# First operands in blocks, the last residuals of the first layer pair in buffers of their own, and a rearranged end in a two-pair graph kernel

## What is computed

```
x = layernorm(x + L0(x, adj));  out = layernorm(x + L1(x, adj))

L0, for each of 2 layers:
  u   = h (h W_left^T)^T on and above the diagonal, h (h W_right^T)^T below it, / sqrt(384)
  p   = exp(u) * adj;  attention = p / (sum(p) + 1e-10)
  ctx = attention @ (h W_lin^T + b);  h = relu((ctx - mean) / (std + 1e-3) * ln_a + ln_b)
L1, for each of 2 layers:
  a   = softmax(h h^T / sqrt(384)) * adj, divided by its row sum
  ctx = upper(a) @ (h Wl^T + bl) + diag(a) * (h Ws^T + bs) + lower(a) @ (h Wr^T + br)
  h   = relu(normalised ctx * ln_w + ln_b)
```

## Time and profile before

| | us |
|---|---|
| median of 3 runs | 1717.54 |
| range of the runs | 1716.96 to 1718.06 |
| the profiled execution | 1716.51 |
| its span, first to last instruction | 1714.9 |
| TensorE busy in the span | 1667.0 (97%) |
| VectorE busy | 1267.7 (74%) |
| ScalarE busy | 948.4 (55%) |
| GpSimd busy | 614.6 (36%) |

### The profile page before, as it was taken

One profiled execution on the slowest core, in us unless ns is written; L12 is line 12 of the kernel. 1 busy time (PEld: TensorE's weight loads), 2 busy tenths in 40 slices (PEclk: granted clock), 3 DMA queues, 4 the chain that ended last, 5 costly groups with the idle time before them and its releaser, 6 DMA issues.

```text
span 1714.9 us, 29860 instructions
## 1 busy us (share of the span) xinstructions
PE 1667.0 (97%) x9664; PEld 1579.3 (92%) x9664; DVE 1267.7 (74%) x2785; ACT 948.4 (55%) x1985; POOL 614.6 (36%) x658
## 2 busy tenths in 40 slices
PE   7999999999999999999989999999999999999994
PEld 6989989899898889889889999999999999999994
DVE  4587685867859578695876877769687696877866
ACT  4545455464554645546556665655655656656653
POOL 5143252432424233243522523525143351523503
PEclk9999999999999999999999999999999999999997
DMA  7015012020300203003013040300304003030101
GB/s 230 1 32 157 6 48 75 24 92 6 104 19 24 92 6 116 6 24 93 21 61 96 22 95 0 102 15 22 95 3 114 1 22 96 22 95 0 64 14 37
DMA packets 108015, 92.19 MB, mean 54 GB/s; under 512 B 63280, under 2 KB 101168, under 8 KB 107952
## 3 DMA queue, kind: packets, MB, share of 16 engines
q1 hardware_dynamic: 107952, 91.51, 18.6%
HBM read 66.33 MB, written 25.17 MB: 53 GB/s over the span
## 4 chain that ended last, share of the span: by engine, by line
PE 51%; issue 32%; POOL 10%; DVE 3%; ACT 2%; SPq 1%; DMA 1%; POOLq 0%; ACTq 0%; DVEq 0%
PE b_work L1157 34%; PE b_work L1170 8%; POOL g_qv_lo L621 3%; POOL b_ht L601 3%; PE b_score_ps L119 3%; PE b_work L372 2%; PE b_score_ps L386 1%; PE b_work L396 1%; POOL g_keep_l L616 1%; POOL g_sigma L630 1%; POOL g_a_nat L617 1%; POOL g_frstd L634 1%; PE b_turn L1114 1%; PE b_score_ps L1133 1%; PE b_score_ps L1130 0%
## 5 line engine op out<-in xcount | busy, mean ns | idle before, releaser
L1157 PE MATMUL b_work<-b_w_hi,b_ht 128*128 128x384 f32 x2304 | 607.0, 338 | 8.3 <-ACT b_work L1256 8.3
L1157 PEld LDWEIGHTS b_work<-b_w_hi,b_ht 128*128 128x128 f32 x2304 | 418.6, 188 | 10.0 <-ACT b_work L1256 9.4
L1157 PE MATMUL b_work<-b_w_lo,b_ht 128*128 128x384 f32 x1152 | 385.9, 335 | 0.0
L372 PE MATMUL b_work<-b_ht,b_w_hi 128*128 128x512 f32 x1152 | 357.7, 392 | 9.5 <-DVE b_w_lo L696 9.5
L372 PEld LDWEIGHTS b_work<-b_ht,b_w_hi 128*128 128x128 f32 x1152 | 216.3, 189 | 51.2 <-issue 9.5
L621 POOL TENSOR_TENSOR g_qv_lo<-g_v_full,g_qv_hi 128x384 fp32r<-128x384 f32 x128 | 133.4, 1062 | 361.0 <-ACT g_qv_hi L495 361.0
L372 PE MATMUL b_work<-b_ht,b_w_lo 128*128 128x512 f32 x576 | 225.8, 392 | 0.0
L1494 DVE TENSOR_TENSOR s_v_lo<-b_work,s_v_hi 128x384 fp32r<-128x384 f32 x256 | 139.3, 554 | 116.1 <-ACT s_v_hi L1262 114.5
L1157 PEld LDWEIGHTS b_work<-b_w_lo,b_ht 128*128 128x128 f32 x1152 | 217.1, 188 | 0.0
L728 DVE TENSOR_TENSOR g_qv_lo<-b_work,g_qv_hi 128x512 fp32r<-128x512 f32 x192 | 128.8, 687 | 111.1 <-ACT g_qv_hi L483 109.2
L396 PE MATMUL b_work<-b_w_hi,b_ht 128*128 128x384 f32 x768 | 206.2, 336 | 0.0
(11 more groups left out here) (142 smaller groups left out, 3247.6 us busy)
## 6 DMA issues: line engine op xcount, KB each, us to landing
b_x_in<-in_x_t SPq DMA_DIRECT2D x16, 768.0 KB, 7.2
g_x_res<-in_x SPq DMA_DIRECT2D x16, 768.0 KB, 7.5
x<-b_z SPq DMA_DIRECT2D x16, 768.0 KB, 3.9
b_x_in<-x SPq DMA_DIRECT2D x64, 192.0 KB, 6.7
s_x_res<-x SPq DMA_DIRECT2D x16, 768.0 KB, 6.9
out<-b_z SPq DMA_DIRECT2D x15, 768.0 KB, 4.1
b_a_tr<-in_adj_t SPq DMA_DIRECT2D x64, 64.0 KB, 3.4
g_a_nat<-in_adj SPq DMA_DIRECT2D x32, 64.0 KB, 2.4
```

The source lines that it names most:

```text
L372: mm = pe.matmul(bank[:], w, h, start=(n == 0), stop=(n == len(pairs) - 1))
L1157: mm = pe.matmul(bank[:, 0:H], h, w, start=(n == 0 and side == 2), stop=(n == len(pairs) - 1), skip_group_check=True)
```

## The change

On the start: the rows of x and W_left come in three blocks each, alternating, with the constants after W_right; ScalarE and VectorE split them block by block; the first three queries are accumulated side by side in three banks, one block of features after the other; W_right is split in three pieces by columns, and query j of W_right waits for its piece alone. Before that TensorE multiplies a tile of zeros ten times. On the hand-over: both `x_res` of the first block outlive it; the sums of the last pass's residuals go there instead of into `z`, and are normalised and stored from there. The residual of stream 0 leaves VectorE's last unit of the first block, gains, shifts, residuals, statistics, offsets, ScalarE's normalisations, the splits of the three weights and SyncE's stores are moved to other places of the second block's first pass (units 0 to 3). On the end: stream 0's cut, row sums and normalisation are done by ScalarE, its addition, statistics and root by GpSimd; the last unit's contexts and variances are taken in halves; the last stores are three.

```
 start, SyncE
-            load_x(0, 0)
+            for k in range(KO):
+                sp.dma_start(stage[0][:, k], weights[0][k * P:(k + 1) * P]).then_inc(first_in[k], 16)
+                sp.dma_start(xt_in[0][:, k], x_t_v[0, 0][:, k]).then_inc(x_loaded[0] if k == KO - 1 else first_in[k], 16)
             for n, w in enumerate(weights):
-                if n == 1:
+                if n == 0:
+                    continue
+                if n == 2:
                     sp.dma_start(const[:], table).then_inc(const_in, 16)
...
 start, TensorE
-            pe.wait_ge(const_in, 16)
-            query(0, 0, 0).then_inc(work_full, 1 + NT)
-            for j in range(1, QB):
+            def first_queries():
+                banks = [work[query_use(0, m) % RING] for m in range(KO)]
+                for k in range(KO):
+                    for n, (w, h) in enumerate(((w_hi, ht_hi), (w_hi, ht_lo), (w_lo, ht_hi))):
...
+                        for m in range(KO):
+                            mm = pe.matmul(banks[m][:], w[:, 0, 0, k, m * P:(m + 1) * P], h[0][:, k, :],
+                                           start=(k == 0 and n == 0), stop=(k == KO - 1 and n == 2))
...
+            pe.wait_ge(zeros_set, 1)
+            for _ in range(10):
+                pe.matmul(score_ps[:, 0, 0, :], prob[:, 0, :], prob[:, 1, :], start=True, stop=True)
+            first_queries()
+            for j in range(KO, QB):
                 query(0, 0, j).then_inc(work_full, 1)
             value(0, 0, 0)
             scores(0, 0, False)
+            pe.wait_ge(const_in, 16)
 start, ScalarE
             for k in range(KO):
-                turn_out(0, 0, k)
-            weight_hi(0)
-            weight_hi(1)
+                first_hi(k)
+            for m in range(KO):
+                second_weight_hi(m)
+            query_hi(0, 0, 0)
             weight_hi(2)
-            query_hi(0, 0, 0)
             for j in range(1, QB):
                 query_hi(0, 0, j)
                 if j < 4:
                     weight_hi(j + 2)
 hand-over, VectorE, last unit of the first block
                 if not more:
-                    add_residual(i, s)
+                    for t in range(NT):
+                        context_stats(i, unit, t, more)
+                    return
 hand-over, VectorE, first unit of the second block
             biased_value(0, 0, 1)
-            gated.gain_and_shift(0)
+            gated.residual(0, 0)
             biased_value(0, 0, 2)
-            gated.gain_and_shift(1)
...
             biased_value(0, 0, 3)
-            gated.gain_and_shift(2)
+            gated.residual(0, 1)
...
             biased_value(0, 0, 6)
-            gated.residual_and_stats((0,))
+            gated.gain_and_shift(0)
...
             biased_value(0, 0, 11)
-            contexts_out(0, 0)
+            gated.gain_and_shift(1)
+            contexts_out(0, 0, first=True)
 hand-over, VectorE, later units (tail is the unit)
+                    if tail == 1 and j < 5:
+                        gated.gain_and_shift(j - 1)
+                    if tail == 2:
+                        gated.final_stats(0, j - 3)
...
 hand-over, ScalarE
             seed(0, 0, 6)
-            gated_normalise(0)
...
             seed(0, 0, 7)
-            weight_hi(0)
...
             copy_part(0, 1)
+            weight_hi(0)
             weight_hi(1)
...
-                if tail:
-                    gated_normalise(1)
...
-                if tail:
-                    weight_hi(2)
                 if more:
                     copy_part(i, unit + 1)
+                if tail == 1:
+                    weight_hi(2)
+                if tail in (2, 3):
+                    gated_normalise(tail - 2)
 hand-over, SyncE
             sp.wait_ge(folded, 1)
-            store_last(0)
             load_weight(0)
             load_weight(1)
             sp.wait_ge(split, 1)
             load_weight(2)
-            store_last(1)
...
                         load_adj(i + 1, s)
+                    if first:
+                        store_last(s)
 end, GpSimd
+            def last_steps(i):
+                s = STREAMS - 1
+                other_residual(i, (0, 1, 2))
+                half_roots(i, 0)
+                other_residual(i, (3,))
+                times_gain(i, s, 0)
+                half_roots(i, 1)
+                plus_shift(i, s, 0)
+                other_statistics()
+                final_roots(i, s, count=0)
 end, ScalarE
+                        other_relu(i)
+                        other_sums(i, (0, 1))
                         normalise(i, unit, range(LAST_GT))
+                        other_sums(i, (2, 3))
+                        other_normalise(i)
+                        final_normalise(i)
 end, VectorE
+                if not more:
+                    contexts_out(i, unit, (0, 1))
+                    half_variances(i, 0)
+                    contexts_out(i, unit, (2,))
+                    last_deviations(i)
+                    contexts_out(i, unit, (3,))
+                    half_variances(i, 1)
+                    return
```

More of the change, by code:

```diff
@@ L1444, in _ @@
             masks(0, 0, first=True)
-            gated_final_roots(0)
             gated_roots()
@@ L1636, in up_to_contexts @@
                     final_var(i, s)
-                contexts_out(i, unit)
+                contexts_out(i, unit, first=tail == 1)
                 if s is not None:
```

348 lines of the change are left out of this document (242 added, 106 removed).

## The result

The changed kernel takes **1708.55 us** (median of 5 runs, 1706.91 to 1708.79); beside it the kernel before took 1717.54 (1715.92 to 1718.06). The ratio is 0.9947, with a 95% interval of 0.9932 to 0.9961. The profiled execution took 1706.91 us, the shortest of the five; its span is 1705.1. I had said 1703.6 and 1698 to 1710: faster, and inside that range, but past the 1700.5 to 1706.5 that I gave the forecast alone, and with half of its terms off.

A forecast was written before the change was run, and what follows sets the result against it. TensorE, busy 1667.0 of 1714.9 us, was taken as the bound, so only its idle 48 us could go. Start +0.4, hand-over -9.8 and tail -4.5 made -13.9 us: median 1703.6 us, own range 1700.5 to 1706.5, widened to 1698 to 1710.

The forecast's parts named there:

- Start: Start of the kernel: earlier matmuls end in a wait, scores not earlier; +0.4 us, bounds -0.2 and +2.4.
- I take 0.2, nearer to the full queue that the row shows: Start: four more DMA issues ahead of the fourth weight delay its landing by 0.2 us, bounds 0 and 1.9.
- Zeros: Start: ten fp32 multiplications by zeros on TensorE take 1 to 4 us, from about 1.3 us; sum unaffected.
- Hand-over: Between the two pairs of layers: TensorE's waits go by moving work; -9.8 us, bounds -6.5 and -11.
- The three waits: Hand-over: first seed wait gives 2.5 us plus 1.5 of slow clock; second (2.06) and third (3.31) give 5.4.
- The small waits that I had given back: Hand-over: new TensorE waits before job 5, job 6 and the scores, from VectorE's order, take back 1.2 us.
- I cost these three and nothing in between: Whole kernel: the change touches only start, hand-over and tail; nothing costed elsewhere.
- nobody needs these before the next pass, so this costs nothing: Hand-over: SyncE's stores wait for normalisations in units 2 and 3, masks and first output queued behind; cost nothing.
- only half of the hand-over is paid: Rival, 15%: TensorE feels 0.75 us of ten moved VectorE operations beside GpSimd; 7 us of gain return, 1710 us.
- Tail: End of the kernel: contexts start 3.7 us earlier, VectorE's chain takes 16.5 us; -4.5 us, bounds -6.5 and -2.5.
- At 0.3 each, nothing: Tail: GpSimd's six small statistics add nothing at 0.3 us each; at 1.1 each they would add 1.5 us.
- the 0.6 us from smaller stores: Tail: three last stores of 192 and 384 KB instead of two of 384 end the kernel 0.6 us earlier.

The follow-up runs named there:

- the kernel again: The changed kernel, unchanged, measured and profiled once more: 1707.97 us against 1716.82 for the kernel before; profiled span 1705.9 us.
- the old start: Changed kernel with the start of the kernel before: one load each of x and first weight, queries one after another, no zeros. 1704.52 us against 1718.33.
- experiments 7 to 9: Changed kernel: ScalarE's queries before weight splits (1707.96 us); GpSimd's blocks before weights too (1704.51); first plus GpSimd's weights and gated statistics later (1701.04; without zeros 1699.02).
- experiment 10: Two changed kernels: early residuals (1706.76 us), and one redundant VectorE wait removed (1706.42), where VectorE's 0.2 us gap ahead of the third softmax unit's maxima was gone.
- early residuals: Changed kernel with VectorE adding gated stream 0's four residuals ahead of the last unit's bank statistics again, as before the change: 1706.76 us against 1717.81.

## Why the prediction was right, and where it was wrong

The sum was -13.9 us; the median moved by -9.0. The direction was right, and so was the sign of each of the three terms that I costed; the size was not: 1708.55 lies inside 1698 to 1710 only because that range was drawn wider than the forecast's own, and the hand-over's surplus of 1.8 us hid as much of the misses. By stretches, against the profile that lies nearest to the median (the kernel again):

- **Start: +0.4 forecast, +2.5 measured** (+1.2 to +2.8 over eight profiles, and 0 with the old start). The mechanism was right, the wait somewhat longer (3 to 5 us forecast, 5.3 to 7.0 measured with the zeros, 4.6 without), and the chain through the fourth weight is what held TensorE: experiments 7 to 9 move it. The term that was mis-sized is the delay of that weight's landing. "I take 0.2, nearer to the full queue that the row shows": the weight came later by about as much as it was issued later, or more (issue 0.8 later and split 1.2 later in the first profile, 1.6 and 2.2 in the second; 0.8 to 1.8 and 1.2 to 2.4 over the eight). My upper bound of 2.4 held four of the eight; the others passed it by up to 0.4. The slow stretch behind the wait cost nothing in the first profile, where I had 0.2.
- **Zeros.** By the earlier trace rows I had put ten of them at 1 to 4 us; they took 4.64, a little over the upper end (4.0 to 4.6 in the other profiles). The profile shows twenty rows, 0.23 us apart, for ten products. By the Trainium skill, "FP8 and Floating Point Precision", TensorE Precision Notes, true fp32 takes four passes; the trace agrees in time: a product of 128 columns took 0.46 us, a little more than one of 512 columns in fp32r at first (0.41). The first real matmul came 0.7 us later than without them (5.73 and 5.07).
- **Hand-over: -9.8 forecast, -11.6 measured** (63.52 + 27.02 against 52.37 + 26.60). The three waits went. For the first this was shown by putting its cause back: 2.4 us for the wait and its clock, where I had 4.0, though only 1.55 of its 2.93 us came back. For the second and third no run did that. The small waits that I had given back (1.2) and the 0.7 of unit 1 mostly didn't come.
- **Third and fourth softmax unit: nothing forecast, +3.75 measured.** This is the step that failed: "I cost these three and nothing in between", and "nobody needs these before the next pass, so this costs nothing", which I had checked for SyncE, GpSimd and ScalarE, not for VectorE. Its four statistics and the variance, 3.5 of the 3.9 us from 922.82 to 926.74 and with them 1.9 of the 3.75 (the rest is the gap of experiment 10), came where I hadn't looked for a due time: ahead of contexts whose successor is a softmax unit of the upper layer, where the maxima and every seed behind them wait. One unit later the successor is a unit of the lower layer, which takes no maxima. The rival "only half of the hand-over is paid" had the cause in VectorE's moved work beside GpSimd. Its place was another, and the hand-over was paid in full, but 1 of the 3.5 us is of its kind: the variance took 1.14 us beside GpSimd's masks and 0.16 with GpSimd idle. That is read from two rows; no run moved the masks.
- **Tail: -4.5 forecast, -4.0 to -4.1 measured** (-2.7 in the first profile). Counted from root 62 the contexts start 3.7 us earlier, as forecast, and VectorE's chain was 16.36 for 16.5. "At 0.3 each, nothing" was low for GpSimd's small steps (0.45 to 0.53, a root 1.23), which cost nothing all the same in ten of twelve profiles, and the 0.6 us from smaller stores didn't come: 5.8 us from offset to end, as before. When a step runs long, the stores queue and 0.9 to 1.3 more is lost.

Sum of the misses: 2.1 - 1.8 + 3.75 + 0.5 = 4.6; the medians differ by 4.95, the rest is in the gated layers' spread of 0.3.

## What to carry to other kernels

When work is moved out of the way, ask of the place it is moved to what the same engine is due to deliver next, and to whom: VectorE's 3.5 us were nearly free beside the fourth unit's values (0.3) and cost 1.9, with the clock 3.8, ahead of a unit that needs a maximum first. A front end that starts earlier is worth nothing until the chain that sets the next stage is reordered on every engine in it; here ScalarE alone moved the scores by 8 us and the time by none. And profile the same kernel twice: two terms of this one (start and tail) differed by 1.4 us each and cancelled.

## What the runs showed of the hardware

The granted clock fell to the lower level, 1.2 GHz, behind waits of 1.89 to 1.93 us in the third unit, and stayed at 2.4 GHz behind waits of 1.57 to 1.61 us at the same place; at 46 us it fell behind 2.88 and not behind 2.40, and at the start it fell behind 5.35. Length alone doesn't decide: behind 1.55 us at 850 (early residuals), where TensorE had stood twice for 0.3 to 0.5 us in the contexts before, it fell, and behind 2.06 and 3.31 us in the kernel before it didn't. The Trainium skill's "TensorE: Matmul & The Clock Gate", Part 1, has idleness restore the throttle; the trace agrees where the clock fell, and shows waits of up to 3.31 us behind which it didn't. A delay of 0.3 us on another engine cost 1.9 through it. In the first microseconds the clock's column doesn't show the slow stretch: it reads 1.00 from 8 to 14 us, where matmuls took 0.41 us each, and 1.00 from 14 on, where they took 0.22.

In two executions of the same program SyncE issued the fourth weight at 15.22 and 16.05, and ScalarE had it at 21.73 and 22.77: a microsecond of spread from the start's transfers alone. GpSimd's operation on 128x4 numbers took 0.45 us in one execution and 2.33 in the other, where VectorE's four residuals (1.95 us) ran beside it. VectorE's own on 128x4 numbers took 1.14 us beside GpSimd's masks and 0.16 without them.
